# The stage that gathers expert results: weights loaded one stage earlier, first rows added first, key norms spread over blocks 1 to 7

## The chip, the cores and the metric

The kernel runs on one core of a Trainium2 chip, as one program with one launch. A core has five engines that run side by side and wait for each other through semaphores: TensorE (PE in the profile: matrix products and transposes, into PSUM), VectorE (DVE), ScalarE (ACT), GpSimd (POOL, which here issues the gathers) and SyncE (SP, which issues the other transfers). The metric is the device time in microseconds of one execution, as the median of several runs; lower is better.

## The reference, cut to what matters

The reference is a stack of four layers on x, 32 sequences of 128 rows of 128 features (4096 tokens). Each layer adds a cross-attention over a context of 77 keys and then a feed-forward part, each behind a layer norm and a gate. The edited stage stands between two of them: it finishes the mixture of experts of layer 1 and makes ready the attention of layer 2.

```python
# layer 1, feed-forward: each token's two best of 8 experts, weighted
out = einsum('ebsd,bse->bsd', eo, comb)
x = x + tanh(g_ffn[1]) * out
# layer 2, attention: what comes ahead of the scores
q = (layernorm(x) @ Wq)      # 16 heads of 8 features
k, v = split(ctx @ Wkv)
q = rmsnorm(q, q_gamma); k = rmsnorm(k, k_gamma)   # over the 8 features of a head
```

The keys and values of layer 3 depend only on the context and layer 3's weights, so the same stage makes them too.

## The kernel before, in words

The program is a row of stages. Each has its own semaphores, written as one block for each engine, and ends in a barrier of all engines, behind which the next stage begins. Inside a stage each engine takes its instructions strictly in the order written.

`chosen_experts` (stage `l1f`) is the stage in front. It runs 39 groups (NG) of 256 rows through the expert that each group belongs to and stores the results to the DRAM tensor `y_rows` (groups of `store`, line 2095). SP loads each group's weights (`wu` line 2088, `wd` line 2091). After the last stores it waits for them (line 2111).

`combine_project` (layer `l2x`, later `l3x`) is the stage that the change is about. The 4096 tokens are 32 tiles of 128 (NT), in 8 blocks of 4 (NBLK, TB). For a block b it does the following.

- POOL gathers for each tile two sets of 128 rows from `y_rows`, one for each of the token's two experts (line 2251), into a ring `yg` of R = 8 tiles. A small addition (`for_load`, line 2249) stands ahead of each tile's pair. From tile 8 on it first waits until the tile eight places back has been added (`added`).
- VectorE adds both sets to `x`, weighted by `share` (lines 2423 and 2427), takes mean and variance (2433, 2436), and makes the scales of the norm from ScalarE's root (2440, 2442).
- ScalarE centres the block with these scales (2365). TensorE transposes it (2287). ScalarE keeps it (2370). TensorE makes the queries (2295). ScalarE squares them (2376). VectorE sums the squares of each head (2446), and the queries are normed (2450, 2454), transposed (2303) and kept (2384), one block behind.
- In between TensorE makes the values of the next block (2279), one piece of layer 3's keys (`later_key`, 2312) and one block of layer 3's values (2318), and ScalarE copies them (2354, 2388, 2392).

Ahead of all blocks stands layer 2's key work. The keys of all 32 sequences are 2464 columns, in NK = 7 pieces of KB = 352. For each piece TensorE makes the keys (2261, PSUM bank 6), ScalarE squares and copies them (2349, 2350), and TensorE adds the squares of each head into one accumulator in bank 7 (2266). ScalarE takes the root (2397), VectorE its reciprocal (2458), and then for each piece TensorE spreads the reciprocal over the features (`key_spread`, 2273, banks 6 and 7 in turn) and VectorE multiplies the keys by it and by gamma (2463). TensorE, ScalarE and VectorE all wait at the very start for `loads`, the layer's weights and gammas (SP, 2238 and 2239). VectorE's order is:

```python
            v.wait_ge(k_rooted, 1)
            v.reciprocal(kroot[:], kroot[:]).then_inc(k_inverted, 1)
            for c in range(NK):
                ...
            for b in range(NBLK):
                add(b)
                stats(b)
```

The next stage (`attention`, line 517 and others) begins when this one has ended on all engines.

## Time and profile before

| what | value |
|---|---|
| time, median of 3 runs | 1444.31 us (1444.18 to 1447.78) |
| the profiled execution: its own time | 1442.63 us |
| its span, first to last instruction | 1440.9 us |
| mean granted TensorE clock | 0.894 of full |
| busy share of PE, DVE, ACT, POOL | 78%, 62%, 54%, 61% |
| the stage of the change, in the trace | 586.1 to 692.7 us |

The profiled execution takes 1.7 us more than its span; the rest of the time lies outside the first and last instruction. The busy shares are means over stages with different limits: the stage in question is a fourteenth of the span and has to be read for itself. Times in the rows below are microseconds from the span's start, and a duration given as "mean ns" is in nanoseconds.

### The profile page before, as it was taken

Reading aid. Unit: us, or ns where it says so; the run is one execution under the profiler, and the core shown is the slowest. Engines: PE = TensorE matmul, PEld = TensorE weight load, DVE = VectorE, ACT = ScalarE, POOL = GpSimd, SP = SyncE. Lnnn points to the kernel's source line nnn. Section 1 sums busy time; section 2 is a strip of 40 time slices with the busy share of each in tenths; the row PEclk is TensorE's granted clock in tenths of the full one; section 3 lists DMA queues with packets and bytes.
Section 4 is the critical chain, followed back from the end, with each engine's and each line's share of the span. In section 5 each row is a group of like instructions: output and inputs, shape, how many; then the busy total and the mean of one; then the engine's idle time right before and its main releaser. Section 6 shows DMA issues by size and latency. Waiting matters only on the chain. (4 is left out here: it accounts for less than half of the span.)

```text
span 1440.9 us, 26005 instructions
## 1 busy us (share of the span) xinstructions
PE 1119.0 (78%) x9096; PEld 817.8 (57%) x9096; DVE 897.0 (62%) x1829; ACT 779.1 (54%) x1506; POOL 876.6 (61%) x1253
## 2 busy tenths in 40 slices
PE   5682588999429999655688868779997796999993
PEld 5431475666428999455466626646665664566662
DVE  6789867998361211165699958868886387344331
ACT  3478466887434455255588866547776352333220
POOL 5200047998316554476599969648886455588875
PEclk9796698999759999887899979989998596999997
DMA  3000001110037888211111000011110103355542
GB/s 114 8 0 0 0 1 54 44 45 5 4 103 215 244 227 222 64 45 44 54 37 37 20 17 1 0 45 35 34 34 2 77 37 109 80 108 109 109 88 22
DMA packets 62021, 89.96 MB, mean 62 GB/s; under 512 B 10363, under 2 KB 33542, under 8 KB 61638
## 3 DMA queue, kind: packets, MB, share of 16 engines
q1 hardware_dynamic: 46086, 70.07, 15.6%
q0 software_dynamic: 15808, 18.24, 7.8%
q8 instruction: 74, 1.21, 0.3%
q14 instruction: 53, 0.43, 0.1%
HBM read 56.96 MB, written 16.12 MB: 51 GB/s over the span
## 5 line engine op out<-in xcount | busy, mean ns | idle before, releaser
L1692 PE MATMUL ps<-topk_up_sb,topk_wu 128*128 128x512 f32 x256 | 121.6, 611 | 1.2 <-DVE topk_rank_a L1798 1.2
L1492 POOL DMA_INDIRECT out<-topk_shared,l3f_route_slots x64 | 102.4, 1600 | 20.4 <-issue 14.6
L147 POOL TENSOR_SCALAR sb_stage<-sb_x,l0f_rstd,l0f_shift 128x128 f32<-128x128 f32 x48 | 24.5, 526 | 145.7 <-DVE l0f_shift L134 145.5
L1579 ACT ACTIVATE topk_ga<-ps 128x512 f32<-128x512 f32 x64 | 38.5, 602 | 125.0 <-PE ps L1692 125.0
L2165 ACT ACTIVATE l1f_g_h<-ps,l1f_g_wd 128x256 f32<-128x256 f32 x156 | 63.6, 475 | 71.8 <-DMA l1f_g_wd<-l1f_W 39.5
L2195 DVE TENSOR_TENSOR l1f_g_y<-ps,l1f_g_wd 128x256 f32<-128x256 f32 x39 | 16.6, 424 | 135.4 <-PE ps L2138 135.4
L1836 DVE TENSOR_TENSOR sb_xnT<-topk_ga,ps 128x512 f32<-128x512 f32 x64 | 44.0, 687 | 89.9 <-ACT topk_ga L1579 89.8
L2077 POOL DMA_INDIRECT l1f_g_xg<-l1f_rows,l1f_route_slots x78 | 75.1, 963 | 17.7 <-issue 12.5
L2129 PE MATMUL ps<-l1f_g_xgT,l1f_g_wu 128*128 128x256 f32 x312 | 75.4, 385 | 1.6 <-ACT l1f_g_xgT L2157 0.9
L2138 PE MATMUL ps<-l1f_g_wd,l1f_g_h 128*128 128x128 f32 x624 | 75.9, 275 | 0.0
L1488 POOL DMA_INDIRECT topk_xg<-l3f_rows,l3f_route_slots x64 | 63.1, 986 | 19.7 <-issue 17.1
L2138 PEld LDWEIGHTS ps<-l1f_g_wd,l1f_g_h 128*128 128x128 f32 x624 | 72.7, 192 | 0.1
L1692 PEld LDWEIGHTS ps<-topk_up_sb,topk_wu 128*128 128x128 f32 x256 | 46.3, 196 | 44.8 <-issue 42.0
L2251 POOL DMA_INDIRECT l2x_c_yg<-l1f_y_rows,sb_dest x64 | 61.2, 956 | 14.8 <-issue 11.1
L1704 PEld LDWEIGHTS ps<-topk_wd,sb_xnT 128*128 128x128 f32 x512 | 59.0, 192 | 10.0 <-DVE sb_xnT L1836 10.0
L2129 PEld LDWEIGHTS ps<-l1f_g_xgT,l1f_g_wu 128*128 128x128 f32 x312 | 57.2, 193 | 8.9 <-ACT l1f_g_xgT L2157 1.6
L1704 PE MATMUL ps<-topk_wd,sb_xnT 128*128 128x128 f32 x512 | 59.9, 275 | 1.4 <-DVE sb_xnT L1836 1.4
L699 DVE TENSOR_REDUCE l3x_rowmax<-ps 128x16 f32<-128x1232 f32 x32 | 46.0, 1439 | 17.4 <-PE ps L591 17.4
L161 ACT ACTIVATE sb_xnT<-ps 128x512 f32<-128x512 f32 x56 | 33.0, 589 | 38.4 <-PE ps L156 38.3
L662 ACT ACTIVATE l1x_pt<-ps 103x512 f32<-103x512 f32 (+1 forms) x96 | 50.8, 608 | 2.6 <-PE ps L603 2.5
L662 ACT ACTIVATE l3x_pt<-ps 103x512 f32<-103x512 f32 (+1 forms) x96 | 50.5, 608 | 2.6 <-PE ps L603 2.6
L662 ACT ACTIVATE l2x_pt<-ps 103x512 f32<-103x512 f32 (+1 forms) x96 | 50.5, 609 | 1.8 <-PE ps L603 1.7
(530 smaller groups left out, 3510.6 us busy)
## 6 DMA issues: line engine op xcount, KB each, us to landing
l1f_g_wd<-l1f_W SPq DMA_DIRECT2D x39, 322.0 KB, 4.0
l1f_g_wu<-l1f_W SPq DMA_DIRECT2D x39, 256.0 KB, 3.5
topk_wu<-l3f_W SPq DMA_DIRECT2D x16, 512.0 KB, 3.7
l1f_y_rows<-l1f_g_y SPq DMA_DIRECT2D x39, 128.0 KB, 3.9
topk_wd<-l3f_W SPq DMA_DIRECT2D x16, 256.0 KB
l1x_vrows<-sb_l0f_up SPq DMA_DIRECT2D x16, 154.0 KB
l2x_vrows<-l2x_vall SPq DMA_DIRECT2D x16, 154.0 KB
l3x_vrows<-l3x_vall SPq DMA_DIRECT2D x16, 154.0 KB
```

The lines of the kernel that those rows point to most:

```text
L662: sc.activation(pt[n % 2][0:rows, c, :, :].rearrange("k g q -> k (g q)"), ps[0:rows, TURN[c], :], ACT.Copy).then_inc(turned_kept, 1)
L699: v.tensor_reduce(rowmax[n % 2][:].rearrange("p (b h) -> p b h", h=HG), scores, X, ALU.max).then_inc(maxed, 1)
L1488: pool.indirect_dma_start(out=xg[g % R][:, i, :], out_offset=None, in_=u["rows"], in_offset=spot(g, i)).then_inc(row_came[g % R], 16)
L1492: pool.indirect_dma_start(out=out_rows, out_offset=spot(g, i), in_=y[g % 2][:, i, :], in_offset=None, compute_op=ALU.add).then_inc(y_added ...
L1692: ins = pe.matmul(ps[:, 2 * (c % 2) + i, :], wu[g % W][:, (i * CX + c) * P:(i * CX + c + 1) * P], xgT[g % 2][:], start=True, stop=True)
L1704: ins = pe.matmul(ps[:, 4 + g % 2, i * P:(i + 1) * P], xh[g % 2][:, c, i * P:(i + 1) * P], wd[g % W][:, c * P:(c + 1) * P], start=(c == 0) ...
L1836: v.tensor_tensor(xh[g % 2][:, c, :], gx[c % 2][:], ps[:, 2 * (c % 2) + 1, :], ALU.mult).then_inc(x_ready, 1)
L2077: pool.indirect_dma_start(out=xg[r][:, i, :], out_offset=None, in_=u["rows"], in_offset=bass.IndirectOffsetOnAxis(ap=u["slots"][:, g * G + ...
L2129: pe.matmul(ps[:, c, 0:GS], wu[g % W][:, c * P:(c + 1) * P], xgT[g % 2][:], start=True, stop=True).then_inc(made, 1)
L2138: ins = pe.matmul(ps[:, 4 + g % 2, i * P:(i + 1) * P], h[g % 2][:, c, i * P:(i + 1) * P], wd[g % W][:, c * P:(c + 1) * P], start=(c == 0), ...
L2165: sc.activation(h[g % 2][:, c, :], ps[:, c, 0:GS], ACT.Gelu, bias=wd[g % W][:, C * P + c:C * P + c + 1]).then_inc(acted, 1)
L2251: pool.indirect_dma_start(out=yg[n % R][:, c, :], out_offset=None, in_=t["y_rows"], in_offset=bass.IndirectOffsetOnAxis(ap=t["dest"][:, c ...
```

## The change

It does four things. SP's loads of layer 2's weights and gammas move from the start of `combine_project` to the end of `chosen_experts`, between its loop and its last three stores, with a wait for them at that stage's end; the waits for `loads` at the start of three engines go. VectorE starts with the adds of block 0; the reciprocal of the key roots stands behind the scales of block 0. The seven key products (`norm_key`) stand one in each of blocks 1 to 7, behind the sum of query squares and ahead of the scales, and TensorE's `key_spread` at the head of the same blocks, in bank 6 alone. `later_key` moves ahead of `query` on TensorE, and ahead of the next block's values on ScalarE, and uses bank 7; later keys and later values now take turns in that bank.

```diff
-def chosen_experts(nc, u, d, stage, E, NG, C):
+def chosen_experts(nc, u, d, stage, E, NG, C, behind):
...
+        loads = s.one("loads")
...
                 if g + 1 in MASK_AT:
                     load_mask(MASK_AT[g + 1])
+            sp.dma_start(u["wstat"][:, 0:512], d[f"{behind}_W"]).then_inc(loads, 16)
+            sp.dma_start(u["cols"][:, 0:2], d[f"{behind}_gamma"]).then_inc(loads, 16)
             for g in range(max(NG - W, 0), NG):
                 store(g)
+            sp.wait_ge(loads, 32)
...
 # combine_project, SP
-            sp.dma_start(w[:, 0:512], d[f"{layer}_W"]).then_inc(loads, 16)
-            sp.dma_start(t["cols"][:, 0:2], d[f"{layer}_gamma"]).then_inc(loads, 16)
             sp.dma_start(t["w_later"][:], d[f"{later}_W"]).then_inc(w_later, 16)
 # TensorE
-            pe.wait_ge(loads, 32)
-
             def key_spread(c):
                 if c == 0:
                     pe.wait_ge(k_inverted, 1)
-                if c >= 2:
-                    pe.wait_ge(k_normed, c - 1)
-                pe.matmul(ps[:, 6 + c % 2, 0:KB], to_features[:, c, :], kroot[:], start=True, stop=True).then_inc(k_spread, 1)
+                if c >= 1:
+                    pe.wait_ge(k_normed, c)
+                pe.matmul(ps[:, 6, 0:KB], to_features[:, c, :], kroot[:], start=True, stop=True).then_inc(k_spread, 1)
 
             def later_key(c):
                 if c == 0:
                     pe.wait_ge(w_later, 16)
-                    pe.wait_ge(k_normed, NK)
+                    pe.wait_ge(k_rooted, 1)
                 else:
-                    pe.wait_ge(kl_kept, c)
-                pe.matmul(ps[:, 6, 0:KB], ...
+                    pe.wait_ge(vl_kept, c)
+                pe.matmul(ps[:, 7, 0:KB], ...
 
             def later_values(b):
-                if b >= 1:
+                pe.wait_ge(kl_kept, min(b + 1, NK))
+                if b >= NK:
                     pe.wait_ge(vl_kept, b)
...
             values(0)
-            for c in range(NK):
-                key_spread(c)
             for b in range(NBLK):
+                if b >= 1:
+                    key_spread(b - 1)
                 turn(b)
                 if b >= 1:
                     turn_query(b - 1)
                 if b + 1 < NBLK:
                     values(b + 1)
-                query(b)
                 if b < NK:
                     later_key(b)
+                query(b)
                 later_values(b)
 # ScalarE
-            sc.wait_ge(loads, 32)
...
                 keep(b)
+                if b < NK:
+                    later_key(b)
                 if b + 1 < NBLK:
                     values(b + 1)
                 square(b)
                 if b >= 1:
                     keep_query(b - 1)
-                if b < NK:
-                    later_key(b)
                 later_values(b)
 # VectorE
-            v.wait_ge(loads, 32)
...
-            v.wait_ge(k_rooted, 1)
-            v.reciprocal(kroot[:], kroot[:]).then_inc(k_inverted, 1)
-            for c in range(NK):
+            def norm_key(c):
                 v.wait_ge(k_spread, c + 1)
                 kc = t["kT"][:, c * KB:(c + 1) * KB]
                 v.wait_ge(k_kept, c + 1)
-                v.scalar_tensor_tensor(kc, kc, gamma_k, ps[:, 6 + c % 2, 0:KB], ALU.mult, ALU.mult).then_inc(k_normed, 1)
+                v.scalar_tensor_tensor(kc, kc, gamma_k, ps[:, 6, 0:KB], ALU.mult, ALU.mult).then_inc(k_normed, 1)
...
             for b in range(NBLK):
                 add(b)
                 stats(b)
                 if b >= 1:
                     sum_query(b - 1)
+                    norm_key(b - 1)
                 scales(b)
+                if b == 0:
+                    v.wait_ge(k_rooted, 1)
+                    v.reciprocal(kroot[:], kroot[:]).then_inc(k_inverted, 1)
                 if b >= 1:
                     norm_query(b - 1)
```

## Rows read from the trace of the kernel before

**Rows 1.** The chain that ended last, by time: its first piece (start, us, what).

```profile
1136.24 3.28 DMA topk_w<-l3s_W
```

**Rows 2.** The table of waits, 584 to 694 us: total us, times, longest.

```profile
DVE sb_x L2423 <- DMA l2x_c_yg<-l1f_y_rows,sb_dest: 19.8, 11, 2.8
...
POOL l2x_c_for_load L2249 <- DVE sb_x L2427: 8.3, 1, 8.3
```

**Rows 3.** Timeline of POOL, 604 to 690 us: start, us, what [idle before <-releaser].

```profile
606.19 0.94 POOL L2251 DMA_INDIRECT l2x_c_yg<-l1f_y_rows,sb_dest  x1 [0.30 <-issue]
615.41 0.23 POOL L2249 TENSOR_TENSOR l2x_c_for_load<-l2x_c_zero 128x1 f32<-128x1 f32 x1 [8.28 <-DVE sb_x L2427]
...
676.73 0.94 POOL L2251 DMA_INDIRECT l2x_c_yg<-l1f_y_rows,sb_dest  x1 [0.31 <-issue]
```

**Rows 4.** Groups by form, 586:607 and 615:678; landing lines of tiles l2x_c_yg, l1f_g_wd.

```profile
L2251 POOL DMA_INDIRECT l2x_c_yg<-l1f_y_rows,sb_dest x16 | 15.2, 952 | 3.8 <-issue 3.7
...
L2251 POOL DMA_INDIRECT l2x_c_yg<-l1f_y_rows,sb_dest x48 | 45.9, 957 | 10.9 <-issue 7.5 <-POOL l2x_c_for_load L2249 3.2
...
DMA to landing us min/median/max: 2.4/2.5/3.3
...
DMA to landing us min/median/max: 3.2/4.0/5.5
```

**Rows 5.** Timeline of all engines, 560 to 625 us: the stage's edge and key work.

```profile
574.71 8.88 SPq L2095 DMA_DIRECT2D l1f_y_rows<-l1f_g_y  x4
...
577.91 1.77 ACT L2165 ACTIVATE l1f_g_h<-ps,l1f_g_wd 128x256 f32<-128x256 f32 x4 [1.69 <-PE ps L2129]
...
586.13 0.35 SPq L2238 DMA_DIRECT2D sb_wstat<-l2x_W  x1
...
586.53 0.43 SPq L2239 DMA_DIRECT2D sb_cols<-l2x_gamma  x1
...
589.13 1.54 PE L2261 MATMUL ps<-sb_ctxT,sb_wstat 128*128 128x352 f32 x2 [6.39 <-DMA sb_cols<-l2x_gamma]
...
604.87 0.55 ACT L2397 ACTIVATE l2x_c_kroot<-ps,sb_eps 128x352 f32<-128x352 f32 x1
...
605.53 2.35 DVE L2458 RECIPROCAL l2x_c_kroot<-l2x_c_kroot 128x352 f32<-128x352 f32 x1 [22.33 <-ACT l2x_c_kroot L2397]
...
613.43 0.58 DVE L2463 SCALAR_TENSOR_TENSOR l2x_kT<-l2x_kT,sb_cols,ps 128x352 f32<-128x352 f32 x1 [0.36 <-PE ps L2273]
613.93 1.13 DVE L2423 SCALAR_TENSOR_TENSOR sb_x<-l2x_c_yg,sb_share,sb_x 128x128 f32<-128x128 f32 x4
```

**Rows 6.** Timeline of all engines, 645 to 700 us: the stage's end.

```profile
679.23 0.35 DVE L2423 SCALAR_TENSOR_TENSOR sb_x<-l2x_c_yg,sb_share,sb_x 128x128 f32<-128x128 f32 x1 [2.18 <-DMA l2x_c_yg<-l1f_y_rows,sb_dest]
...
682.58 1.65 ACT L2365 ACTIVATE l2x_c_xn<-sb_x,l2x_c_shift,l2x_c_rstd 128x128 f32<-128x128 f32 x4
...
692.05 0.69 ACT L2384 ACTIVATE sb_xnT<-ps,sb_cols 128x512 f32<-128x512 f32 x1 [2.06 <-PE ps L2303]
693.84 6.37 SPq L517 DMA_DIRECT2D l2x_vrows<-l2x_vall  x8
```

**Rows 7.** Timelines of ScalarE and TensorE, 617 to 675 us: centring, squares, later work.

```profile
634.12 1.65 ACT L2365 ACTIVATE l2x_c_xn<-sb_x,l2x_c_shift,l2x_c_rstd 128x128 f32<-128x128 f32 x4 [0.23 <-DVE l2x_c_shift L2442]
...
638.71 0.60 ACT L2376 ACTIVATE l2x_c_qsq<-ps 128x512 f32<-128x512 f32 x1 [0.30 <-PE ps L2295]
...
641.40 1.65 ACT L2365 ACTIVATE l2x_c_xn<-sb_x,l2x_c_shift,l2x_c_rstd 128x128 f32<-128x128 f32 x4 [0.20 <-DVE l2x_c_shift L2442]
...
651.51 1.65 ACT L2365 ACTIVATE l2x_c_xn<-sb_x,l2x_c_shift,l2x_c_rstd 128x128 f32<-128x128 f32 x4
...
658.39 0.60 ACT L2376 ACTIVATE l2x_c_qsq<-ps 128x512 f32<-128x512 f32 x1 [0.89 <-PE ps L2295]
...
647.16 1.05 PE L2312 MATMUL ps<-sb_ctxT,l3x_w 128*128 128x352 f32 x2
648.05 1.04 PE L2318 MATMUL ps<-l3x_w,sb_ctxT 128*77 128x128 f32 x8
```

**Rows 8.** Windows: us, busy by engine PE, PEld, DVE, ACT, POOL, then PEclk, DMA share, GB/s.

```profile
630.00:640.00 10.00, 7.02 (x57) 6.19 (x55) 6.50 (x29) 7.20 (x16) 8.40 (x12) 1.00 0.23 56
...
650.00:660.00 10.00, 6.62 (x34) 6.13 (x34) 5.14 (x20) 5.02 (x12) 8.10 (x13) 0.66 0.19 48
```

More of the change, by code:

```diff
@@ L2207, in combine_project @@
         s = Sems(nc, ctx, layer + "c")
-        loads, halved, added, stat, var_ready, rooted, recip, scaled, normed, turned, kept = (
-            s.one("loads"), s.one("halved"), s.one("added"), s.one("stat"), s.one("var_ready"), s.one("rooted"), s.one("recip"),
+        halved, added, stat, var_ready, rooted, recip, scaled, normed, turned, kept = (
+            s.one("halved"), s.one("added"), s.one("stat"), s.one("var_ready"), s.one("rooted"), s.one("recip"),
             s.one("scaled"), s.one("normed"), s.one("turned"), s.one("kept"))
@@ L2308, in later_key @@
                     pe.wait_ge(w_later, 16)
-                    pe.wait_ge(k_normed, NK)
+                    pe.wait_ge(k_rooted, 1)
                 else:
-                    pe.wait_ge(kl_kept, c)
-                pe.matmul(ps[:, 6, 0:KB], t["w_later"][:, 128:256], t["ctxT"][:, c * KB:(c + 1) * KB], start=True, stop=True).then_inc(kl_made, 1)
+                    pe.wait_ge(vl_kept, c)
+                pe.matmul(ps[:, 7, 0:KB], t["w_later"][:, 128:256], t["ctxT"][:, c * KB:(c + 1) * KB], start=True, stop=True).then_inc(kl_made, 1)
             def later_values(b):
-                if b >= 1:
+                pe.wait_ge(kl_kept, min(b + 1, NK))
+                if b >= NK:
                     pe.wait_ge(vl_kept, b)
@@ L2387, in later_key @@
                 sc.wait_ge(kl_made, c + 1)
-                sc.activation(t["kT_later"][:, c * KB:(c + 1) * KB], ps[:, 6, 0:KB], ACT.Copy).then_inc(kl_kept, 1)
+                sc.activation(t["kT_later"][:, c * KB:(c + 1) * KB], ps[:, 7, 0:KB], ACT.Copy).then_inc(kl_kept, 1)
             def later_values(b):
@@ L2462, in _ @@
                 v.wait_ge(k_kept, c + 1)
-                v.scalar_tensor_tensor(kc, kc, gamma_k, ps[:, 6 + c % 2, 0:KB], ALU.mult, ALU.mult).then_inc(k_normed, 1)
+                v.scalar_tensor_tensor(kc, kc, gamma_k, ps[:, 6, 0:KB], ALU.mult, ALU.mult).then_inc(k_normed, 1)
+            assert NK == NBLK - 1
             for b in range(NBLK):
@@ L2849, in build @@
                 t["y_rows"] = nc.dram_tensor("l1f_y_rows", (NG1 * PAIR * P, D), F32).ap()
-                routed("l1f", 8, NG1, PAIR, lambda u: top_two(nc, u, 8, 5), True, lambda u: chosen_experts(nc, u, d, "l1f", 8, NG1, 4), two_choices=True)
+                routed("l1f", 8, NG1, PAIR, lambda u: top_two(nc, u, 8, 5), True, lambda u: chosen_experts(nc, u, d, "l1f", 8, NG1, 4, "l2x"), two_choices=True)
             t["kT_later"], t["vall_later"] = keys_and_values(held, "l3x")
```

## The prediction, made before the changed kernel was run

> **What bounds the kernel now.** I read the page first, then its chain of work that ended last. That chain can be followed back only to 1136 us [rows 1], so it says nothing of the stage that the diff edits; I take that stage for itself. It lies between two barriers of all engines, and the next stage starts everything anew 1.1 us after ScalarE's last instruction here [rows 6]. So whatever moves the stage's last instruction moves all that follows, one for one, unless a later stage runs differently by its start.
>
> Inside the stage, the table of waits has two lines that matter [rows 2]. POOL, which issues the gathers, stood idle once, for 8.3 us, for VectorE's second add of a tile. VectorE stood idle 19.8 us for gathered rows, in 11 pieces. The timeline of POOL shows when [rows 3]: two gathers for each tile until the ring of eight tiles is full at 606.19 + 0.94 = 607.1 us, then nothing until 615.41, then again without a break until 677.7. From 615.41 to 677.67 it issues 24 tiles: 62.3 / 24 = 2.60 us each, 10.4 us for a block of four. Everything after the stall is this rate: the last tile's rows reach VectorE at 679.23, after it had waited 2.18 us for them [rows 6]. So the stage is the issue of 64 gathers, plus one stall, plus a tail from 679.23 to 692.7.
>
> Why the stall is there stands in VectorE's rows [rows 5]: its first instruction of the stage is the reciprocal of the key roots at 605.53, then the seven key products until 614.0, and only then the adds that free a ring place. And the roots came at 604.87 because the key chain started only at 589.13, when the weights had landed that SP asked for at 586.13.
>
> **The change part by part.**
>
> Adds ahead of key work. VectorE can add block 0 as soon as its rows are there. Tile 3's second gather is issued by 586.3 + 4 x 2.6 = 596.7, less its own 0.95, and lands 2.5 us after its issue [rows 4]: 598.3. One first add (0.34) and four second ones (1.1) make 599.8. POOL needs its first free place at 607.1, a margin of 7 us. It needs the next block's first place four tiles later, at 617.5; tiles 4 to 7 land by 608.7, and ahead of their adds stand scales of block 0 and the reciprocal (2.35 us), which waits for the key roots. Those come at 605.4 even without earlier weights, so the reciprocal is over by 607.9, and this margin is 7 us too. So the whole stall goes: **-8.28 us** for every later gather [rows 3]. The last rows then come at 679.23 - 8.28 = 670.95.
>
> A rule speaks against counting all of it. The gathers that were issued with VectorE idle took 952 ns each, 16 of them, and the 48 beside its adds 957 ns [rows 4]; one of 0.94 us lay wholly inside the 2.35 us reciprocal [rows 3, 5]. By the rows, 16 newly covered gathers cost 16 x 5 ns = 0.1 us. The Trainium skill (SBUF — State Buffer, section on the two separate sides) says that VectorE and GpSimd share a port pair under an exclusive lock, so that GpSimd cannot write descriptors while certain VectorE instructions hold it. By that rule, with each of the 16 held for one add of 0.34 us, 5.4 us would be given back; the trace does not agree for these shapes.
>
> Weights loaded a stage earlier. SP's two issues (0.35 and 0.43 us) go between its store at 574.71 and the next, which waits for VectorE at about 577.9, so they delay no store. The stage in front has one load under way then, issued just ahead of that store and needed by ScalarE's last activations at 577.91 [rows 5]; such loads landed in 3.2 to 5.5 us [rows 4]. Another 256 KB beside it may make it 0 to 1 us later, of which the last group can hide some, since VectorE waits for TensorE there and not for ScalarE: I take 0, and keep 1 us for the range. The added wait stands before the wait for the last stores, which SP has anyway. What it brings: key chain from about 586.4 instead of 589.13, -2.7 us. But the gathers don't depend on it, so on the path it brings 0; its cover is POOL's issue, and if the keys were 7 us later than now the stall would begin to come back.
>
> Key products spread over blocks 1 to 7. Each is 0.58 us on VectorE, seven in all [rows 5], and now one follows each sum of query squares, ahead of the scales. In the last block this place stands on the tail: after the sum of squares come only the scales, and then the centring on ScalarE at 682.58 [rows 6]. The root that the scales need is already there, so the product is paid in full: **+0.58 us**. The other six lie in time when VectorE would wait for rows. TensorE's seven spreads move into the blocks (up to 1.05 us each, by a later key's product of the same shape [rows 7]) right behind the values of the block in front, where TensorE has 3 to 4 us idle before the next transposes.
>
> Later keys before the query. TensorE now does the later key product ahead of the queries, and ScalarE copies it earlier. It took 1.05 us at the lower clock, and the next product began 0.9 after it (647.16, 648.05 [rows 7]); at full clock I estimate 0.6, between half of that and all of it. This lengthens the loop from one centring to the next: centring to end of square took 634.12 to 639.31 = 5.2 us with TensorE's granted clock at 1.00, and 651.51 to 658.99 = 7.5 us in a stretch at 0.66 [rows 7, 8], mostly at the lower of 2.4 and 1.2 GHz. Add the later key, 0.6 to 0.9, and the end of square to the next centring (639.31 to 641.40 = 2.1, of which one copy of 0.4 has moved ahead; VectorE's sum, product and scales take 1.65 of it): 1.8. The loop is 5.2 + 0.6 + 1.8 = 7.6 to 7.5 + 0.9 + 1.8 = 10.2 us. The gathers give a block each 10.4. So the loop stays just inside.
>
> Where the loop starts counts as well. Block 0 is centred after key roots and values on ScalarE, at about 604; block 1 at most 10.2 later, 614.2. Block 7's centring is due, by gathers, at 682.58 - 8.28 + 0.58 = 674.9. Between lie six loops: they keep up if one takes (674.9 - 614.2) / 6 = 10.1 us or less. With a mixed clock I expect about 9.5, so the gathers decide.
>
> Sum: -8.28 + 0.58 = **-7.7 us**, 0.1 of port contention inside the rounding. The stage's last instruction goes from 692.7 to 685.0, the span from 1440.9 to 1433.2, and the profiled execution's time from 1442.63 to 1434.9. The median of the runs shown is 1444.31, 1.7 above the profiled one; I put the change against that: **1436.6 us**. Following work may start in another state of the clock: the loop above differs by 2.3 us between the two stretches of before (7.5 and 5.2), and the tail holds less than one loop; I keep 2 us either way for this and the stages behind.
>
> **The rivals.**
>
> *The loop becomes the bound.* If a block takes 10.9 us instead of at most 10.2, because the waits between TensorE and ScalarE add up at the lower clock, block 7 is centred at 614.2 + 6 x 10.9 = 679.6 instead of 674.9: gain 3.0, time 1441.3. For it: the sum at 1.2 GHz is 0.2 us from the period, and the gaps that let the clock fall stay. Against: no block of before ran wholly at 1.2 GHz. The Trainium skill (TensorE: Matmul & The Clock Gate, part 1) says that the array is throttled by default and released by activity; by that rule, blocks paced by gathers would be the slow ones, as the granted clock here agrees (1.00 before the gathers bind, 0.66 after).
>
> *The key product's wait on TensorE decides, and it is slower than before.* VectorE's scales of each block now stand behind a product that waits for TensorE's spread, which is queued behind later keys, queries and later values of the block in front. Now these end at 648.05 + 1.04 = 649.1, some 2 us before the scales of that block, whose centring follows at 651.51 [rows 7]; the spread eats up to 1.05 of it. If each round trip is a further 1.2 us late, the loop is 11.4 and the gain gone: 614.2 + 6 x 11.4 = 682.6, where block 7 was centred before. At 12.4 us it is 688.6, or +6.0: 1450.3.
>
> *The gathers do not come sooner.* If the adds of block 0 still wait, or each newly covered gather is held by an add (the 5.4 us above), the gain is 0 to 2.3: 1442.0 to 1444.3. Only the first add's order could do this, and it stands first in the queue now.
>
> *More than the sum*: the clock comes out better in tail and next stages, another 2 to 3 us: 1434.
>
> **How the numbers follow.** The sum as forecast, 1434.5 to 1439, 0.64; more than the sum 0.09; loop bound 0.12; no sooner 0.10; slower by the spread's wait 0.05. About 0.3% (4.3 us) can be told from no change, so faster means below 1440.0: the first two, and half of the loop's and a little of the gathers': 0.81. Within: 0.14. Slower: 0.05. For the range I leave out the slower case and the upper end of no gain, and go 4 us below: 1432.5 to 1443.0.
>
> **What would show it.** POOL's gathers without the 8.3 us idle, the last one starting near 668.4, or the same 2.60 us a tile. VectorE's first instruction an add near 590, not a reciprocal. Waits of VectorE for rows in blocks 1 to 7, not for spreads. Centring in block 7 near 674.9. The stage's end near 685. If the first spread or the sum of squares ends long waits of VectorE instead, the loop decides; if the stage in front ends later than 586.1, the moved loads cost. The prediction is wrong if the gathers' pitch grows, or if a later stage takes the gain back.

## The result, and the profile after

The changed kernel takes 1435.19 us (median of 5 runs, 1434.61 to 1437.28), the kernel before beside it 1444.31 us (5 runs, 1442.84 to 1447.78). The ratio is 0.9938 with a 95% interval of 0.9922 to 0.9954: 9.0 us less, between 6.6 and 11.3. The ratio, here and in the tables below, is not quite the quotient of the two medians; for one kernel below (ring16_b) the medians are 4.8 us apart where the ratio makes 6.4. One execution of another kernel (loads_only_b) took 1723.34 us at a granted clock of 0.63: its median of 1441.82 counts it, its ratio does not.

The profiled execution of the changed kernel was the longest of its five: 1437.28 us, with a span of 1435.6 us against 1440.9 before. These 5.3 us can't be read off whole: the stage in question already starts 2.92 us later in this trace. That shift was there before the moved loads were issued at 578.10: VectorE's last four products of the stage in front, from 576.65 on, begin 2.90 to 2.91 us later than before. So I measure the stage from POOL's first instruction to the end of ScalarE's last. Before it is 106.61 us, from 586.13 to 692.05 + 0.69 = 692.74 [rows 6]; after it is 589.05 to 687.16 + 0.69 = 687.85, or 98.80 us. **The stage is 7.81 us shorter.** What lies behind it is 0.4 us shorter.

POOL's timeline, 584 to 700 us (start, us, what [idle before <-releaser]), answers to [rows 3]:

```profile
589.05 0.10 POOL L2246 MEMSET l2x_c_zero<- 128x1 f32 x1 [19.07 <-POOLq L63]
...
606.64 0.94 POOL L2253 DMA_INDIRECT l2x_c_yg<-l1f_y_rows,sb_dest  x1 [0.30 <-issue]
607.61 0.20 POOL L2251 TENSOR_TENSOR l2x_c_for_load<-l2x_c_zero 128x1 f32<-128x1 f32 x1
...
609.22 0.94 POOL L2253 DMA_INDIRECT l2x_c_yg<-l1f_y_rows,sb_dest  x1 [0.30 <-issue]
610.19 0.20 POOL L2251 TENSOR_TENSOR l2x_c_for_load<-l2x_c_zero 128x1 f32<-128x1 f32 x1
...
671.28 0.95 POOL L2253 DMA_INDIRECT l2x_c_yg<-l1f_y_rows,sb_dest  x1 [0.30 <-issue]
```

The ninth tile's first instruction, at 610.19, waited 8.28 us in [rows 3]; here it follows the eighth tile's second gather (609.22 + 0.94) without a wait. The last gather starts 82.23 us into the stage, where it was 90.60.

The table of waits, 584 to 694 us, answers to [rows 2]; POOL's wait for VectorE is no longer in it, and VectorE's for rows has grown from 19.8 to 43.0 us:

```profile
DVE sb_x L2420 <- DMA l2x_c_yg<-l1f_y_rows,sb_dest: 43.0, 18, 7.4
```

The groups by form, POOL, 589 to 690 us: one gather costs 954 ns in the mean of all 64, where the two groups in [rows 4] make (15.2 + 45.9) / 64 = 0.955 us.

```profile
L2253 POOL DMA_INDIRECT l2x_c_yg<-l1f_y_rows,sb_dest x64 | 61.1, 954 | 14.8 <-issue 11.1 <-POOL l2x_c_for_load L2251 3.3
```

VectorE's timeline, 574 to 625 us, the order that the change makes:

```profile
585.69 0.42 DVE L2199 TENSOR_TENSOR l1f_g_y<-ps,l1f_g_wd 128x256 f32<-128x256 f32 x1 [1.36 <-PE ps L2142]
593.50 0.35 DVE L2420 SCALAR_TENSOR_TENSOR sb_x<-l2x_c_yg,sb_share,sb_x 128x128 f32<-128x128 f32 x1 [7.39 <-DMA l2x_c_yg<-l1f_y_rows,sb_dest]
...
601.72 1.13 DVE L2424 SCALAR_TENSOR_TENSOR sb_x<-l2x_c_yg,sb_share,sb_x 128x128 f32<-128x128 f32 x4
...
606.16 2.34 DVE L2470 RECIPROCAL l2x_c_kroot<-l2x_c_kroot 128x352 f32<-128x352 f32 x1
```

VectorE now begins with an add. Block 0's four second adds are over by 601.72 + 1.13 = 602.85; POOL wants the first place that they free at 610.19. That is a margin of 7.3 us, where I had 7.

The timeline of all engines, 660 to 700 us, answers to [rows 6]:

```profile
673.78 0.35 DVE L2420 SCALAR_TENSOR_TENSOR sb_x<-l2x_c_yg,sb_share,sb_x 128x128 f32<-128x128 f32 x1 [2.18 <-DMA l2x_c_yg<-l1f_y_rows,sb_dest]
...
676.16 0.65 DVE L2443 TENSOR_REDUCE l2x_c_qsum<-l2x_c_qsq 128x64 f32<-128x512 f32 x1
...
676.73 0.57 DVE L2458 SCALAR_TENSOR_TENSOR l2x_kT<-l2x_kT,sb_cols,ps 128x352 f32<-128x352 f32 x1
...
677.62 1.65 ACT L2364 ACTIVATE l2x_c_xn<-sb_x,l2x_c_shift,l2x_c_rstd 128x128 f32<-128x128 f32 x4 [0.43 <-DVE l2x_c_shift L2439]
...
687.16 0.69 ACT L2383 ACTIVATE sb_xnT<-ps,sb_cols 128x512 f32<-128x512 f32 x1 [2.06 <-PE ps L2303]
```

The stage splits into three pieces at the last rows (673.78) and the last centring (677.62):

| piece | before, us | after, us | difference |
|---|---|---|---|
| stage start to last rows | 93.10 | 84.73 | -8.37 |
| last rows to block 7's centring | 3.35 | 3.84 | +0.49 |
| block 7's centring to the end | 10.16 | 10.23 | +0.07 |

The last piece is not the same in every execution. Over all fourteen traces of this study it takes 9.33 to 10.91 us, in kernels that don't differ there too: 9.33 in the second traces of both kernels. So a difference of less than a microsecond between two stage lengths says little by itself; the pieces ahead of it say more.

SP's timeline, 566 to 592 us, shows the two moved loads in the stage in front:

```profile
577.62 0.43 SPq L2096 DMA_DIRECT2D l1f_y_rows<-l1f_g_y  x1
578.10 0.47 SPq L2109 DMA_DIRECT2D sb_wstat<-l2x_W  x1
578.61 0.47 SPq L2110 DMA_DIRECT2D sb_cols<-l2x_gamma  x1
580.84 5.66 SPq L2096 DMA_DIRECT2D l1f_y_rows<-l1f_g_y  x3
```

From VectorE's last product of that stage (585.69) to the stage's start (589.05) it is 3.36 us, against 3.35 in the trace of before. The moved loads cost the stage in front nothing.

Last, the loop, that is the work of one block from its centring on ScalarE, over TensorE, ScalarE and VectorE, to the next block's centring. ScalarE's timeline, 600 to 660 us: the key roots, block 0, and the steps to blocks 2 and 3:

```profile
604.62 0.55 ACT L2396 ACTIVATE l2x_c_kroot<-ps,sb_eps 128x352 f32<-128x352 f32 x1
...
606.28 1.65 ACT L2364 ACTIVATE l2x_c_xn<-sb_x,l2x_c_shift,l2x_c_rstd 128x128 f32<-128x128 f32 x4 [0.44 <-DVE l2x_c_shift L2439]
...
615.65 1.65 ACT L2364 ACTIVATE l2x_c_xn<-sb_x,l2x_c_shift,l2x_c_rstd 128x128 f32<-128x128 f32 x4 [0.43 <-DVE l2x_c_shift L2439]
...
624.63 0.30 ACT L2357 ACTIVATE l2x_c_rstd<-l2x_c_mv,sb_eps_ln 128x4 f32<-128x4 f32 x1 [2.14 <-DVE l2x_c_mv L2433]
...
625.97 1.65 ACT L2364 ACTIVATE l2x_c_xn<-sb_x,l2x_c_shift,l2x_c_rstd 128x128 f32<-128x128 f32 x4 [0.42 <-DVE l2x_c_shift L2439]
...
635.13 0.29 ACT L2357 ACTIVATE l2x_c_rstd<-l2x_c_mv,sb_eps_ln 128x4 f32<-128x4 f32 x1
...
636.32 1.65 ACT L2364 ACTIVATE l2x_c_xn<-sb_x,l2x_c_shift,l2x_c_rstd 128x128 f32<-128x128 f32 x4 [0.43 <-DVE l2x_c_shift L2439]
```

Block 0 is centred 606.28 - 589.05 = 17.23 us into the stage, where it was 31.8. Centring to centring is 10.32 and 10.35 us in the last two steps, the gathers' own period. Ahead of 624.63 ScalarE had stood idle 2.14 us for statistics, that is for rows. Ahead of 635.13 it had not stood idle at all, which looks as if there the loop had become the bound. VectorE's timeline, 629 to 638 us, decides it:

```profile
632.48 0.35 DVE L2420 SCALAR_TENSOR_TENSOR sb_x<-l2x_c_yg,sb_share,sb_x 128x128 f32<-128x128 f32 x1 [0.73 <-DMA l2x_c_yg<-l1f_y_rows,sb_dest]
...
634.58 0.36 DVE L2433 BATCH_NORM_AGGREGATE l2x_c_mv<-l2x_c_st 128x2 f32<-128x6 f32 x4
634.86 0.65 DVE L2443 TENSOR_REDUCE l2x_c_qsum<-l2x_c_qsq 128x64 f32<-128x512 f32 x1
635.43 0.57 DVE L2458 SCALAR_TENSOR_TENSOR l2x_kT<-l2x_kT,sb_cols,ps 128x352 f32<-128x352 f32 x1
635.92 0.17 DVE L2437 RECIPROCAL l2x_c_rstd<-l2x_c_rstd 128x4 f32<-128x4 f32 x1
```

VectorE waited for the block's last rows until 632.48 and then had no idle time up to the centring. The root that the reciprocal needs was ready at 635.13 + 0.29 = 635.42, and VectorE came to it at 635.92. So the rows set this centring too, and the loop had 0.5 us to spare: by these rows I estimate the loop itself at 10.35 - 0.50 = 9.85 us here. The granted clock of this stretch was 0.87; a stretch at 0.66 throughout doesn't occur in this trace:

```profile
630.00:640.00 10.00, 7.00 (x44) 5.94 (x43) 5.79 (x22) 5.37 (x12) 8.37 (x12) 0.87 0.21 54
```

### The profile page after: what moved, and what is told of

Its sections match the earlier page's. It is cut to its first block and busy times, and to the rows that moved or that the text cites. A ratio compares the mean times of both kernels' runs of the same rounds, so it can differ in the third digit from the quotient of the medians.

```text
span 1435.6 us, 26005 instructions
## 1 busy us (share of the span) xinstructions
PE 1119.5 (78%) x9096; PEld 818.7 (57%) x9096; DVE 895.1 (62%) x1829; ACT 779.2 (54%) x1506; POOL 876.7 (61%) x1253
## 3 DMA queue, kind: packets, MB, share of 16 engines
q1 hardware_dynamic: 46086, 70.07, 15.7%
## 5 line engine op out<-in xcount | busy, mean ns | idle before, releaser
L2253 POOL DMA_INDIRECT l2x_c_yg<-l1f_y_rows,sb_dest x64 | 61.1, 954 | 14.8 <-issue 11.1
L1049 PE MATMUL ps<-sb_xnT,sb_l0f_wT 128*128 128x512 f32 x96 | 45.6, 628 | 8.9 <-ACT sb_l0f_up L968 7.0
```

Source lines behind the costliest of these rows:

```text
L1049: ins = pe.matmul(ps[:, 3 * (j % 2) + c, :], wT[:, (first + c) * P:(first + c + 1) * P], t["xnT"][:, j * BLK:(j + 1) * BLK], start=True, s ...
L2253: pool.indirect_dma_start(out=yg[n % R][:, c, :], out_offset=None, in_=t["y_rows"], in_offset=bass.IndirectOffsetOnAxis(ap=t["dest"][:, c ...
```

## The experiments

Two theories were to be told apart. Mine: the gathers' issue is the stage's bound, so the gain is POOL's stall and nothing else, less the key product on the tail (the tail is what follows the last rows). The rival: the blocks' loop is the bound or close to it, so the gain comes from block 0's early start and from the key work taken out of the way. Three groups of kernels ran on three chips, each with the kernel before beside it. Each kernel has one trace; the stage lengths and pieces in the tables are those of that one execution.

### First group: four kernels on a chip with pauses

On the first chip the kernel before takes 1484.22 us (1478.47 to 1489.36), 40 more than on the others. The edits were these.

ring16, on the kernel before:

```diff
-    R = 8
+    R = 16
```

> The kernel before with a ring of 16 tiles in place of 8, nothing else changed. Stage length is taken from POOL's first instruction of the stage to the end of ScalarE's last: 106.6 us before, 98.8 after the change. Theory (the gain is the one stall of the gathers at a full ring): tile 8 needs no free place until tile 16, the 8.28 us idle of POOL is gone though VectorE's order is untouched, the tail has no key product in it, so the stage takes 106.6 - 8.3 = 98.3 us and the time falls by 8.3. Rival 1 (the order of the key work on VectorE is what counts, since block 0 starts late): the stage stays at 106.6. Rival 2 (the blocks' own loop becomes the bound once rows are there early): centring of block 0 at 617.95, then loops of 7.3 us at full clock give block 7 at 617.95 + 8.9 + 6 x 7.3 = 670.6, ahead of the rows; only with loops above 8.0 would it be later than 98.3.

loads_only, the moved loads alone on the kernel before:

```diff
+            sp.dma_start(u["wstat"][:, 0:512], d[f"{behind}_W"]).then_inc(loads, 16)
+            sp.dma_start(u["cols"][:, 0:2], d[f"{behind}_gamma"]).then_inc(loads, 16)
             for g in range(max(NG - W, 0), NG):
                 store(g)
+            sp.wait_ge(loads, 32)
...
-            sp.dma_start(w[:, 0:512], d[f"{layer}_W"]).then_inc(loads, 16)
-            sp.dma_start(t["cols"][:, 0:2], d[f"{layer}_gamma"]).then_inc(loads, 16)
```

> The kernel before with only the weights and gammas loaded by the stage in front. Theory: before, the stall ends when the key work ends, so key work 3.1 us earlier (as in the trace after) shortens the stall from 8.3 to 5.2 us and the stage from 106.6 to 103.5: the part that brings nothing inside the full change brings 3 us alone. Rival (the loads bring nothing anywhere, or delay the last groups of the stage in front): stage 106.6 and the time within 1 us of before, or the edge of the stage in front later than 3.35 us behind its last VectorE instruction.

late_loads, the full change without this part: the same lines the other way round, and VectorE waits for the loads only ahead of its first key product:

```diff
             def norm_key(c):
+                if c == 0:
+                    v.wait_ge(loads, 32)
```

> The changed kernel with the loads back at the start of the stage. Theory: the gathers do not depend on them, so the gathers go through without the stall; block 0 is centred 3 us later, which the loops of blocks 1 and 2 win back at full clock (natural loop 7.6 to 9.4 us against a period of 10.35), and the stage takes 98.8 us. Rival (the loop at the lower clock is as long as the period, so lateness is never won back): up to 3 us remain, stage up to 101.8 us.

norm_last, on the changed kernel:

```diff
                 if b >= 1:
                     sum_query(b - 1)
-                    norm_key(b - 1)
                 scales(b)
...
                     norm_query(b - 1)
+                    norm_key(b - 1)
```

> The changed kernel with each key product behind the norm of the queries, as VectorE's last work of a block, instead of ahead of the scales. Theory: in block 7 it then lies in VectorE's 4.6 us of waiting for the squares, so the tail gives back the product's 0.5 us: from the last rows to the centring 3.35 us as before and not 3.84, stage 98.3 us. Rival (the product was hidden and the tail is longer for another reason, such as the squares being late): centring stays 3.84 us behind the last rows and the stage at 98.8.

| kernel | median, us | ratio to before, 95% | stage, us | POOL's waits over 5 us |
|---|---|---|---|---|
| ring16 | 1490.10 | 1.0035 (1.0015 to 1.0055) | 141.45 | 6.01, 8.59 |
| loads_only | 1481.32 | 0.9970 (0.9953 to 0.9988) | 131.28 | 7.79, 8.83, 7.59 |
| late_loads | 1479.70 | 0.9961 (0.9944 to 0.9978) | 129.69 | 6.51, 7.01, 9.54 |
| norm_last | 1483.71 | 0.9990 (0.9974 to 1.0006) | 134.68 | 10.60, 7.65 |

None of the four met its expectation; the stage lengths are 28 to 43 us above them. Even norm_last, which has all of the change but one instruction's place, needs 134.68 us where the changed kernel needed 98.80. In time, the interval of norm_last holds 1: on this chip nearly the whole change brings nothing that can be told from no change. The reason stands in its timelines of ScalarE and TensorE, 610 to 636 us:

```profile
609.55 1.65 ACT L2364 ACTIVATE l2x_c_xn<-sb_x,l2x_c_shift,l2x_c_rstd 128x128 f32<-128x128 f32 x4 [0.44 <-issue]
618.82 0.60 ACT L2369 ACTIVATE sb_xnT<-ps 128x512 f32<-128x512 f32 x1 [7.62 <-issue]
632.89 0.46 ACT L2387 ACTIVATE l3x_kT<-ps 128x352 f32<-128x352 f32 x1 [13.48 <-DMA sb_graw<-g_ffn]
...
611.25 1.11 PE L2287 MATMUL ps<-sb_ident,l2x_c_xn 128*128 128x128 f32 x4 [8.28 <-ACT l2x_c_xn L2364]
...
613.86 0.87 PE L2312 MATMUL ps<-sb_ctxT,l3x_w 128*128 128x352 f32 x2
...
633.41 1.99 PE L2319 MATMUL ps<-l3x_w,sb_ctxT 128*77 128x128 f32 x8 [11.86 <-ACT l3x_kT L2387]
```

ScalarE copies the later key at 632.89, though TensorE had made it by 613.86 + 0.87 = 614.7; it stood 13.48 us with its input ready. Just before, it had stood 7.62 us, of which 6.5 with the transposes made (611.25 + 1.11 = 612.36). TensorE and VectorE then wait for it, VectorE's adds come late, and POOL's ring fills. Pauses of 6.5 to 15.7 us are in all four traces of this chip, in this stage and in the last one. In ring16, TensorE and VectorE are slow beside them: from the end of the reciprocal (611.15) to the end of the seventh key product (636.18) they take 25 us, where the kernel before takes 6.1 (607.88 to 614.01 [rows 5]). The last stage is about 10 us longer (314.4 to 317.0 us against 301.1 to 307.1 on the other chips); all others take what they take elsewhere. On this chip the pauses are the bound and not the gathers' rate, so these four kernels decide nothing about my sum. What the pauses are is left open, below.

### Second group: the parts of the bound, on a second chip

The kernel before takes 1443.42 us here. Two kernels are the two originals again, as a scale for the rest, without an edit.

> The kernel before once more, for a trace on the same chip as the three runs beside it. The four runs ahead of this one came from a chip on which the kernel before takes 1484 us and not 1444, and their traces show ScalarE standing still 10 to 15 us at a time with its inputs ready, only while gathers are in flight. Theory A (these pauses are the chip's, whatever the kernel): where the time is near 1484 the stage takes about 130 us in this kernel too, with such pauses, and where it is near 1444 it takes 106.6 with none over 5 us outside the first wait. Theory B (the edits brought the pauses): none in this kernel on either chip.

> The changed kernel once more, same chip as its neighbours. On a chip without the pauses: stage 98.8 us, time 8 us under before. On a chip with them, theory A says that the pauses are the bound and what remains of the 7.8 us depends on where they fall: gain 0 to 6 us, POOL's first stall gone but others of 6 to 10 us in its place, each behind a pause of ScalarE. Rival: the gathers bound the stage there as well and the gain is the same 7.8 us.

no_step, on the changed kernel, makes the gathers cheaper: POOL's addition between two tiles, and the wait for it, are gone.

```diff
-                pool.wait_ge(load_step, n + 1)
-                pool.tensor_tensor(for_load[:], zero[:], zero[:], ALU.add).then_inc(load_step, 1)
```

> The changed kernel without the small addition that POOL does ahead of each tile's two gathers. It costs 0.20 us and the pause behind it 0.15 in a period of 2.59, so gathers alone would need 2.24 to 2.5 us a tile. Theory (the gathers' issue bounds the blocks, with the blocks' own loop just behind it at 7.6 to 10.35 us): on a chip without pauses the period falls to 9.0 to 10.0 us a block only while TensorE's clock is full; at the lower clock the loop of about 10.3 takes over. Stage between 98.8 - 32 x 0.1 = 95.6 and 98.8 - 6, time 2 to 6 us under the changed kernel, and VectorE's waits for rows (43.0 us after the change) shrink. Rival (the loop is already the bound): stage stays at 98.8.

bulk_keys, on the changed kernel, takes the spreading away but keeps the adds first: all seven products stand behind block 0's scales. TensorE makes the seven spreads in one piece ahead of block 0's transposes, in two PSUM banks as before, and layer 3's first key waits for the last product; VectorE's part of the edit:

```diff
                 if b >= 1:
                     sum_query(b - 1)
-                    norm_key(b - 1)
                 scales(b)
                 if b == 0:
                     v.wait_ge(k_rooted, 1)
                     v.reciprocal(kroot[:], kroot[:]).then_inc(k_inverted, 1)
+                    for c in range(NK):
+                        norm_key(c)
```

> The changed kernel with all seven spreads and key products in one piece behind the scales and the reciprocal of block 0, in two banks as before, instead of one in each block. Theory (what counts is that block 0's adds come first; the spreading only has to keep clear of the ring): the products end at about 5.5 us behind the reciprocal, 3 us after the last rows of block 1, still 5 us ahead of POOL's need of a place, so no stall comes back; block 0's transposes wait 8 us for TensorE, which loops at full clock win back by block 7; the tail has no product in it: stage 98.3 us on a chip without pauses. Rival (the spreading is what gained): the late start of block 0 is kept to the end or the stall returns, stage 101 to 107 us.

| kernel | median, us | ratio to before, 95% | stage, us | last gather, into the stage |
|---|---|---|---|---|
| before_again | 1442.82 | 0.9996 (0.9975 to 1.0018) | 107.01 | 91.75 |
| after_again | 1437.72 | 0.9942 (0.9920 to 0.9965) | 98.69 | 82.86 |
| no_step | 1432.76 | 0.9928 (0.9903 to 0.9952) | 97.08 | 80.21 |
| bulk_keys | 1436.43 | 0.9949 (0.9930 to 0.9968) | 99.03 | 82.69 |

The pair repeats: a stall of 9.38 us is gone, the last rows come 8.81 us sooner in the stage, block 7's centring follows them 3.84 us later instead of 3.35, and the stage is 8.32 us shorter. In the kernel before no pause like those of the first chip is to be seen here; whether it has them on that chip its time of 1484 us only suggests, as there is no trace of it from there.

no_step shifts the last gather by 2.65 us against after_again. POOL's timeline of it, 655 to 671 us, shows what a tile then costs:

```profile
667.68 0.94 POOL L2251 DMA_INDIRECT l2x_c_yg<-l1f_y_rows,sb_dest  x1 [0.30 <-issue]
668.93 0.94 POOL L2251 DMA_INDIRECT l2x_c_yg<-l1f_y_rows,sb_dest  x1 [0.30 <-issue]
```

From start to start 1.25 us, so 2.50 a tile against 2.58 with the addition (607.61 to 610.19 in the first trace of the changed kernel): the addition's 0.2 us was mostly paid out of the 0.3 us that lie ahead of a gather anyway. From block 2 on the centrings come each 10.07 to 10.26 us and no longer 10.30 to 10.66 as in after_again. VectorE still waits 40.4 us for rows. So the gathers were the bound, and they remain it when they are a little faster. Block 7 is centred 2.85 us sooner than in after_again (86.51 us into the stage, not 89.36); the tail behind it takes 1.24 us more (10.57, not 9.33), which leaves 1.6 us. So the theory held and its numbers did not: it had a stage of 92.8 to 95.6 us, with 0.1 us or more off each tile, and blocks of 9.0 to 10.0 us at full clock; the rows give 0.08 a tile, and 2.85 us up to the last centring. The rival, a stage that stays at 98.8, is out by those 2.85 us. The time is 5.0 us below after_again by the medians, more than the stage explains; in this trace the last stage, which has no edit, is 3.4 us shorter (301.1 against 304.5).

bulk_keys decides on the spreading. ScalarE's timeline, 600 to 690 us, the centrings of blocks 0 to 4:

```profile
606.29 1.65 ACT L2364 ACTIVATE l2x_c_xn<-sb_x,l2x_c_shift,l2x_c_rstd 128x128 f32<-128x128 f32 x4 [0.44 <-DVE l2x_c_shift L2439]
620.28 1.65 ACT L2364 ACTIVATE l2x_c_xn<-sb_x,l2x_c_shift,l2x_c_rstd 128x128 f32<-128x128 f32 x4 [0.19 <-DVE l2x_c_shift L2439]
629.41 1.65 ACT L2364 ACTIVATE l2x_c_xn<-sb_x,l2x_c_shift,l2x_c_rstd 128x128 f32<-128x128 f32 x4 [0.21 <-DVE l2x_c_shift L2439]
636.88 1.65 ACT L2364 ACTIVATE l2x_c_xn<-sb_x,l2x_c_shift,l2x_c_rstd 128x128 f32<-128x128 f32 x4 [0.21 <-DVE l2x_c_shift L2439]
646.33 1.65 ACT L2364 ACTIVATE l2x_c_xn<-sb_x,l2x_c_shift,l2x_c_rstd 128x128 f32<-128x128 f32 x4
```

Block 1 is centred 13.99 us after block 0, 4 us late, but the next steps of 9.13, 7.47 and 9.45 us win it back, POOL never stalls, and the stage is 0.34 us from after_again. The product is off the tail as expected (3.35 us from the last rows to the centring), but the stage is 99.03 us and not 98.3, because what follows the centring took 10.45 us, against 9.33 in after_again. It was enough that the adds of block 0 stand ahead of the key work; a gain of the spreading itself is not to be seen.

### Third group: each part alone, and the best version, on a third chip

The kernel before takes 1444.55 us here. ring16_b, loads_only_b and late_loads_b are the edits of the first group again, without that chip's pauses.

> The kernel before with a ring of 16 tiles, once more, since its first trace came from the chip with ScalarE's pauses. On a chip near 1443 us for the kernel before: theory (the stall at the full ring is the gain) says that POOL never stands, the last gather starts about 82.3 us into the stage as after the change (90.6 and 91.8 before), the stage takes 98.3 us and the time is 8 us under before, with VectorE's order untouched. Rival (the order of the key work is what counts): stage 106.6. Near 1484 us the pauses decide and the run says nothing on this.

> The kernel before with only the weights loaded by the stage in front, once more. On a chip near 1443: theory says the stall of 8.3 to 9.4 us falls to 5.2 to 6.3 and the stage from 106.8 to 103.6, time -3.1 us. Rival (nothing): stage 106.8.

> The changed kernel with the loads back in the stage, once more. On a chip near 1443: theory says block 0 is centred about 20.4 us into the stage and not 17.2, the loops win it back, no stall of POOL over 1 us, stage 98.8 (98.7 to 99.0 in the two traces of the changed kernel and the one with keys in one piece), so the moved loads bring 0 in the full change. Rival (lateness stays): up to 102.

last_no_step joins norm_last and no_step: the tail's product behind the tail's scales, and POOL's addition gone.

> The changed kernel with both of the edits that looked worth keeping: each key product as VectorE's last work of its block, and no small addition ahead of the gathers. On a chip near 1443: the addition alone gave a stage of 97.1 (0.07 us a tile, 10.15 us a block), the product off the tail gives 0.5 more: centring of block 7 3.35 us behind the last rows and not 3.84, stage 96.6 us, time 10 us under before and 2 under the changed kernel. Rival (the squares are late for the tail's sum, or the loop binds): the 0.5 us do not come, stage 97.1 or more.

| kernel | median, us | ratio to before, 95% | stage, us | last gather, into the stage |
|---|---|---|---|---|
| ring16_b | 1439.72 | 0.9956 (0.9937 to 0.9974) | 105.57 | 82.30 |
| loads_only_b | 1441.82 | 0.9981 (0.9959 to 1.0003) | 104.42 | 87.99 |
| late_loads_b | 1434.99 | 0.9924 (0.9899 to 0.9950) | 99.56 | 82.93 |
| last_no_step | 1429.77 | 0.9901 (0.9863 to 0.9938) | 96.34 | 79.61 |

**loads_only_b** came near its expectation: a stall of 5.04 us for 5.2 to 6.3, and a stage of 104.42 for 103.6. Its time can't be told from no change, as the interval holds 1. POOL's timeline, 604 to 616 us:

```profile
612.86 0.23 POOL L2251 TENSOR_TENSOR l2x_c_for_load<-l2x_c_zero 128x1 f32<-128x1 f32 x1 [5.04 <-DVE sb_x L2423]
```

The stall was 8.28 us: the keys start earlier, VectorE comes to its adds earlier, and POOL waits that much less. In the full change the same part brings next to nothing: late_loads_b centres block 0 at 19.90 us instead of 17.23, and its stage is 0.76 us longer than the changed kernel's 98.80, where I expected 0, with ratios that can't be told apart (0.9924 and 0.9938).

**ring16_b** missed its expectation, and this was the most useful run. A ring of 16 takes the whole stall away and leaves all other orders as before, so on my theory the stage should have come down by about 8 us. The last gather does come 8.30 us sooner. The stage is 1.04 us shorter. That is next to the rival's 106.6, by which the order of the key work counts because block 0 starts late. VectorE's timeline, 660 to 690 us, shows the last rows' adds:

```profile
671.67 1.13 DVE L2423 SCALAR_TENSOR_TENSOR sb_x<-l2x_c_yg,sb_share,sb_x 128x128 f32<-128x128 f32 x4
...
678.35 0.69 DVE L2446 TENSOR_REDUCE l2x_c_qsum<-l2x_c_qsq 128x64 f32<-128x512 f32 x1 [3.44 <-ACT l2x_c_qsq L2376]
```

All four first adds run in a row with no wait for rows; what VectorE waits for now is the loop (3.44 us for the squares). ScalarE's timeline, 615 to 692 us, with the centrings of block 0 and of blocks 4 to 6, and under it the windows, the clock behind the five busy times:

```profile
617.96 1.65 ACT L2365 ACTIVATE l2x_c_xn<-sb_x,l2x_c_shift,l2x_c_rstd 128x128 f32<-128x128 f32 x4 [0.44 <-DVE l2x_c_shift L2442]
...
650.28 1.65 ACT L2365 ACTIVATE l2x_c_xn<-sb_x,l2x_c_shift,l2x_c_rstd 128x128 f32<-128x128 f32 x4 [0.20 <-DVE l2x_c_shift L2442]
...
660.42 1.65 ACT L2365 ACTIVATE l2x_c_xn<-sb_x,l2x_c_shift,l2x_c_rstd 128x128 f32<-128x128 f32 x4 [0.20 <-DVE l2x_c_shift L2442]
...
670.61 1.65 ACT L2365 ACTIVATE l2x_c_xn<-sb_x,l2x_c_shift,l2x_c_rstd 128x128 f32<-128x128 f32 x4 [0.20 <-DVE l2x_c_shift L2442]
```

```profile
630.00:640.00 10.00, 7.04 (x57) 6.16 (x54) 7.16 (x31) 7.27 (x16) 8.09 (x13) 1.00 0.20 51
...
650.00:660.00 10.00, 7.17 (x34) 6.55 (x34) 5.21 (x21) 5.25 (x13) 8.21 (x12) 0.66 0.20 52
```

Block 0 is centred 31.81 us into the stage as in the kernel before. Blocks 2 and 3 follow at 7.29 us each at a clock of 1.00, and I had counted on that for the rest; but then the step is 8.93, and once the clock is 0.66 the loop alone, in the order of before, takes 10.14 to 10.21 us, so that little is won back. My expectation for ring16 had named this case (only with loops above 8.0 us), and the one for ring16_b left it out. So the stall and block 0's late start were two limits with nearly the same end. Taking away one leaves the other: in these traces the change needed both its halves, gathers that never stop and a block 0 that is centred at 17.23 us.

The measured gain of ring16_b, 6.4 us by its ratio (3.8 to 9.1), is more than its stage shows, and by time alone it can't be told from the full change. The traces tell where the rest lies in the profiled execution. Its stage starts at 586.15 us, as in the kernel before (586.13), and all that follows the stage is 3.7 us shorter; 3.1 of it lie in the stage `sine_ffn`, which takes 103.35 us here and 106.49 there. No edit of this study touches that stage, and it takes 102.0 to 106.7 us in the fourteen traces (103.8 in before_again). So most of the rest is no work of the edit. Whether the 1.04 us of the stage hold for the other executions of ring16_b as well is not shown.

**last_no_step** has the lowest median of the study and met its expectation of the stage, 96.6 us; in time its interval overlaps that of no_step. The timeline of VectorE, 665 to 684 us:

```profile
667.44 0.35 DVE L2418 SCALAR_TENSOR_TENSOR sb_x<-l2x_c_yg,sb_share,sb_x 128x128 f32<-128x128 f32 x1 [2.04 <-DMA l2x_c_yg<-l1f_y_rows,sb_dest]
...
672.08 0.57 DVE L2456 SCALAR_TENSOR_TENSOR l2x_kT<-l2x_kT,sb_cols,ps 128x352 f32<-128x352 f32 x1
677.03 0.69 DVE L2441 TENSOR_REDUCE l2x_c_qsum<-l2x_c_qsq 128x64 f32<-128x512 f32 x1 [4.38 <-ACT l2x_c_qsq L2373]
```

The last key product now lies in the 4.95 us between the query's product and the last sum of squares, where VectorE would wait anyway; it still waits 4.38 us there. Block 7's centring comes at 670.78, 3.34 us after its last rows: the 0.49 us of the changed kernel's tail are back. The time is 14.8 us under before by the medians, where I had 10; the stage has no more than 10.3 to 10.7 of them. Its gathers also took 948 ns in the mean, no_step's 958; over 64 that is the 0.6 us by which the last one is sooner. In no_step ten gathers took 0.99 to 1.07 us, here four took over 0.97; why is not shown.

## Why the prediction was right

I forecast 1436.6 us, in a range of 1432.5 to 1443.0, and 7.7 us less than before; measured were 1435.19 and a difference of 9.1 between the medians. The sum's terms, by the traces:

- **The stall, -8.28.** Measured -8.37 up to the last rows. The stall is gone whole, and the gathers' pitch is what it was: the last gather starts at 82.23, as 90.60 - 8.28 = 82.32 says. In the second pair it is 82.86 where 91.75 - 9.38 = 82.37 would be.
- **The last key product on the tail, +0.58.** Measured +0.49, and taken back by last_no_step when the product goes behind the scales.
- **Moved loads, 0.** 3.36 us at the stage's edge against 3.35. Key roots 15.57 us into the stage instead of 18.74, which is -3.17 where I had -2.7. What that is worth was right for this change (late_loads_b: 0.8 us at most) and is not a property of the loads: alone, on the kernel before, they took 3.2 us off the stall and 2.2 off the stage (loads_only_b, against 106.61).
- **Port contention, at most 0.1.** Gathers of 954 ns, where [rows 4] give 952 and 957; the one that starts at 606.64 lies wholly inside the reciprocal of 606.16 to 608.50 and takes 0.94 us. (Of the 16 gathers that I called issued with VectorE idle, the last two lay partly or wholly inside the reciprocal of before.) The means of the ten traces without pauses lie between 948 and 963 ns, 1 us over 64 gathers, and both ends are kernels that add beside the gathers. So no gather was held for an add, and the 5.4 us of that rival are out. I had that price from a rule of the Trainium skill (SBUF — State Buffer, the section on the two separate sides), but the section speaks of VectorE's 2-port modes, and of instructions with two SBUF inputs only against GpSimd work that reads SBUF; that adds like these hold the gathers' descriptors back it does not say, and the traces show no such thing.
- **The loop, 7.6 to 10.2 us, inside the period of 10.4.** Each step from block 1 on took 10.28 to 10.35 us, the gathers' period, with the loop, estimated at 9.85 us, inside it. The rival of the loop as the bound needed more than 10.4 and had none of it here; it is what bounds ring16_b, with the order of before. The margin was as small as I had it: 0.2 us forecast at the lower clock, 0.5 read off at a clock of 0.87. How this loop comes out with the clock at 0.66 over several blocks is not shown; from 610 to 680 us it stayed between 0.79 and 0.89, which I had not forecast, and in that there is some luck. The 0.66 that I gave for the blocks of before that the gathers pace holds for the windows from 650 and from 670 us; those from 640 and from 660 us are at 0.83.
- **Spreads that VectorE waits for**, the slower rival: the product follows the sum of squares at once in the rows above, at 635.43 and at 676.73.

One statement of the working doesn't hold in general. I wrote that after the stall everything is the gathers' rate, and took the loop only as a condition. ring16_b shows that it was a second limit hidden in the kernel before: without the stall, and with block 0 as late as it was, the stage ended 7 us later than the sum says (105.57 us of stage against 106.61 - 8.28 = 98.33). My check of where the loop starts (block 0 at about 604, block 1 by 614.2), made for the changed kernel alone, is what carried the forecast; on the clock of the traces of before these were 603.4 and 612.7.

The stage explains 7.8 us of the 9.1. The other 1.3 lie inside the interval of 6.6 to 11.3, and I don't assign them. That the time came within 1.4 us of the forecast is in part luck, since a stage without an edit varies by up to 4.7 us between traces (`sine_ffn`); the stage's own 7.81 us against 7.7 are the better test.

## What to carry to other kernels

When a ring stalls, look at who frees its first place and what stands ahead of that in its own queue; but then ask what the consumer's loop can do at the lower clock, since a deeper ring cures the stall alone, and in its trace here the stage gained 1 us of the 8. Parts of a change don't add: the moved loads take 2 us off the stage alone and at most 0.8 once the adds come first. Work that nobody waits for belongs behind the instruction that the next engine waits for, not ahead of it, in the last block above all, where every microsecond is paid in full.

## What the runs showed of the hardware that was not expected

**Pauses on one chip.** On the first chip ScalarE stood still for 6.5 to 15.7 us at a time, nearly all of it with its input ready, in this stage and the last one, and the same kernel took 1484.22 us instead of 1443.42 to 1444.55 on the others. Both stages gather. But `chosen_experts` gathers too, and it took 161.1 to 162.9 us on that chip and 160.3 to 162.8 on the others. Some pauses ended 2.9 to 3.8 us after POOL's last gather ahead of a full ring, at least one ended before POOL stopped, so that the gathers cause them is not shown. The instruction queues moved five packets in this stage in each of the four traces, as in the kernel before without pauses, and not at the pauses' ends. A deeper ring, which lets POOL issue longer without a stop, was 0.35% slower there and 0.44% faster on the third chip. What the pauses are stays open.

**The loop and the clock.** In one trace (ring16_b) the loop from centring to centring takes 7.29 us at a granted clock of 1.00 and 10.14 to 10.21 us at 0.66. TensorE's busy time is nearly the same in both stretches, 7.04 and 7.17 of 10 us, but it is that of 57 matrix products in one and of 34 in the other. So the clock can't be told from how busy TensorE looks.

**Drift.** Two traces of the same kernel differ by 2.1 us at this stage's start (586.13 and 588.24 for the kernel before), and by 2.7 in the length of `sine_ffn` (106.49 and 103.80). A gain of a few microseconds has to be read from the stage's own length, not from the span.
